# A graph attention block on one core: a step over eight elements instead of four, V through a second buffer, x in a ring of four

## The reference

```python
q, k, v = (heads(x @ W + b) for W, b in ((Wq, bq), (Wk, bk), (Wv, bv)))   # 6 heads of 64
scores = einsum('bhqd,bhkd->bhqk', q, k) / 8
probs = softmax(scores + where(adj, 0.0, -9e15)[:, None])
ctx = einsum('bhqk,bhkd->bhqd', probs, v)          # heads side by side again
x = x + ctx @ Wf + bf
out = (x - mean(x)) / sqrt(var(x) + 1e-5)          # over the 384 features
```

## Time and profile before

| | before |
|---|---|
| median of 3 runs | 1001.83 us (1001.54 to 1002.15) |
| profiled execution | 1002.12 us, span 1000.3 us |
| busy: PE / weight loads / DVE / ACT / POOL | 991.7 / 900.2 / 706.7 / 589.5 / 633.1 us |
| matmuls | 7690 |
| granted TensorE clock, mean | 0.999 |
| DMA | 178.08 MB, 178 GB/s, queue of SP busy 64.8% of 16 engines' span |

### The profile page before, as it was taken

How to read it: one execution, slowest core, us unless ns; L and a number is a source line. 1 busy time by engine, 2 the same in 40 slices (tenths; PEclk the granted TensorE clock), 3 DMA queues, 4 the chain that set the end, 5 groups by cost and what they waited for, 6 DMA issues and landing times.

```text
span 1000.3 us, 27877 instructions
## 1 busy us (share of the span) xinstructions
PE 991.7 (99%) x7690; PEld 900.2 (90%) x7690; DVE 706.7 (71%) x2760; ACT 589.5 (59%) x2130; POOL 633.1 (63%) x653
## 2 busy tenths in 40 slices
PE   9999999999999999999999999999999999999997
PEld 8788999889999889998899988999988999889997
DVE  5676766867668667677676686766777766867667
ACT  4766545675446665466654566554666545675556
POOL 2446657567566576575675765766656657567566
PEclk9999999999999999999999999999999999999999
DMA  8776676666776666766667666667666676665543
GB/s 186 175 196 167 172 210 189 178 163 171 199 193 186 168 170 175 218 172 182 161 176 204 188 178 169 173 183 207 181 173 168 171 215 181 176 171 160 160 151 104
DMA packets 344780, 178.08 MB, mean 178 GB/s; under 512 B 228784, under 2 KB 328752, under 8 KB 344752
## 3 DMA queue, kind: packets, MB, share of 16 engines
q1 hardware_dynamic: 343264, 176.77, 64.8%
q10 hardware_dynamic: 1488, 0.98, 0.3%
HBM read 103.35 MB, written 74.32 MB: 178 GB/s over the span
## 4 chain that ended last, share of the span: by engine, by line
PE 97%; ACT 1%; DVE 0%; DMA 0%; issue 0%; POOL 0%; SPq 0%; POOLq 0%; DVEq 0%
PE work_ps L427 16%; PE work_ps L429 15%; PE work_ps L428 15%; PE scores_ps L446 9%; PE scores_ps L466 9%; PE scores_ps L427 7%; PE scores_ps L429 7%; PE scores_ps L428 7%; PE work_ps L508 6%; PE scores_ps L508 6%; ACT probs L866 1%; DMA x_in<-in_x 0%; ACT qT L894 0%; PE scores_ps L545 0%; PE scores_ps L556 0%
## 5 line engine op out<-in xcount | busy, mean ns | idle before, releaser
L866 ACT ACTIVATE probs<-probs,neg_max 128x128 f32<-128x128 f32 x768 | 297.5, 392 | 87.9 <-DVE neg_max L676 87.9
L1038 POOL TENSOR_TENSOR probs<-probs,inv_sum 128x768 f32<-128x768 f32 x128 | 188.3, 1471 | 152.0 <-DVE inv_sum L699 152.0
L676 DVE CUSTOM_DVE_ANT_0 probs<-scores_ps,mask_bias 128x128 f32<-128x128 f32 x768 | 167.3, 286 | 127.9 <-PE scores_ps L446 127.2
L875 ACT COPY v_sb<-work_ps 128x384 f32<-128x384 f32 x128 | 61.3, 479 | 263.4 <-PE work_ps L429 263.4
L1033 POOL TENSOR_SCALAR y_sb<-y_sb,mean_var,rstd 128x384 f32<-128x384 f32 x120 | 198.4, 1653 | 21.5 <-POOL rstd L1023 21.5
L1023 POOL TENSOR_TENSOR rstd<-var_eps,minus_half 128x1 f32<-128x1 f32 x128 | 86.5, 676 | 168.5 <-DVE var_eps L720 168.5
L866 ACT ACTIVATION_READ_ACCUMULATOR probs<-probs,neg_max 128x1 f32 x768 | 146.9, 191 | 0.0
L1017 POOL TENSOR_TENSOR x_bias<-x_in,bias_row 128x384 f32<-128x384 f32 x128 | 128.9, 1008 | 7.7 <-DVE bias_row L829 7.7
L427 PE MATMUL scores_ps<-wf_hi,cT_hi 128*128 128x384 f32 x384 | 129.3, 337 | 0.0
L429 PE MATMUL scores_ps<-wf_hi,cT_lo 128*128 128x384 f32 x384 | 129.2, 336 | 0.0
L428 PE MATMUL scores_ps<-wf_lo,cT_hi 128*128 128x384 f32 x384 | 129.1, 336 | 0.0
(11 more groups left out here) (94 smaller groups left out, 2068.1 us busy)
## 6 DMA issues: line engine op xcount, KB each, us to landing
p_out<-p_turned SPq DMA_DIRECT2D x125, 384.0 KB, 2.8
pT<-p_out SPq DMA_DIRECT2D x500, 96.0 KB, 2.8
x_in<-in_x SPq DMA_DIRECT2D x128, 192.0 KB, 2.9
x_blocks<-in_x SPq DMA_DIRECT2D x372, 64.0 KB, 2.3
out<-y_sb SPq DMA_DIRECT2D x120, 192.0 KB, 2.1
adj_u<-in_adj SPq DMA_DIRECT2D x32, 64.0 KB, 2.1
out<-xT SPq DMA_DIRECT2D x4, 192.0 KB, 2.7
out<-qT SPq DMA_DIRECT2D x4, 192.0 KB, 1.9
```

Of the source, the lines that this page charges most:

```text
L676: last = nc.vector.tensor_tensor_reduce(out=probs[:, e, h, :], in0=scores_ps[:, score_cols(e, h)], in1=mask_bias[:, e, :], scale=-SCALE, s ...
L866: last = nc.scalar.activation(probs[:, e, h, :], probs[:, e, h, :], ACT.Exp, bias=neg_max[:, e, h:h + 1], scale=-1.0, accum_out=row_sum[:, ...
L1038: nc.gpsimd.tensor_tensor(probs[:, e, :, :], probs[:, e, :, :], inv_sum[:, e, :].unsqueeze(2).broadcast_to([P, HEADS, SEQ]), ALU.mult).the ...
```

## The change

A step now works on a set of eight elements (16 sets, one per turn of the loop). On PE it goes: scores of elements 0 to 3, two halved q/k products, scores of 4 to 7, two more halved products (four of twelve in all), the contexts of all eight, eight whole q/k products, then output products and V in fours. A context bank now holds one head pair of four elements instead of all heads of one, so `round_ctx` and `split_ctx` handle 128x512 tiles, three for four elements. x is transposed, rounded and split two elements at a time, the sums of elements 0 to 3 are inverted by one instruction. V is copied out of PSUM into `v_next` and moved to `v_sb` by four DMA transfers a step (`move_v`). `x_in` has four slots instead of eight, and POOL adds the bias in place; `x_blocks` has one slot instead of two. `y_sb` keeps four slots. In the last set nothing is transposed by PE, and its order on all engines is new. The pieces of the diff below are, in this order: buffers and banks, SP's new transfer, what the first scores of a set wait for on PE, PE's step, DVE's sum with x, POOL's step (its start and its end), and DVE's order in the last set.

```diff
-        x_in = sb("x_in", [P, RING, HID])
-        x_bias = sb("x_bias", [P, RING, HID])
-        x_blocks = sb("x_blocks", [P, TURN, KC, GROUP * BLOCKS, BLK])
+        x_in = sb("x_in", [P, GROUP, HID])
+        x_blocks = sb("x_blocks", [P, KC, GROUP * BLOCKS, BLK])
+        v_next = sb("v_next", [P, SET, HID])
+        v_sb = sb("v_sb", [P, SET, HID])
...
+OUT_BANKS = (2, 5, 6, 1, 7, 0, 3, 4)
+SCORE_PAIRS = (((0, 3), (1, 4), (2, 5)), ((1, 4), (2, 5), (6, 7)))
...
+            def move_v(s, q):
+                part = slice(2 * q, 2 * q + 2)
+                if q == 0:
+                    past(sp, v_copied, s * SET + SET - 1)
+                    past(sp, ctx_done, s * 2 * KC - 1)
+                sp.dma_start(v_sb[:, part, :], v_next[:, part, :]).then_inc(v_moved, DMA)
...
+                    elif pair == 0:
+                        past(pe, y_added, n - SET - 2)
+                    elif pair == 1:
+                        past(pe, y_added, n - SET - 1)
+                        past(pe, v_copied, n + 4)
...
+            def step(s):
+                if halved(s + 1):
+                    scores(s, 0)
+                    for j in (0, 1):
+                        qk_halves(s + 1, j)
+                scores(s, 1)
+                if halved(s + 1):
+                    for j in (2, 3):
+                        qk_halves(s + 1, j)
+                    for half in range(2):
+                        ctx_group(s - 1, half)
+                for j in range(HALVED if halved(s + 1) else 0, 2 * NJ):
+                    qk_product(s + 1, j)
+                for half in range(1 if is_step(s, LAST - 1) else 2):
+                    if not is_step(s, 0):
+                        for e in range(half * GROUP, (half + 1) * GROUP):
+                            out_product(s - 1, e)
+                    for e in range(half * GROUP, (half + 1) * GROUP):
+                        v_product(s + 1, e)
...
+            def add_residual(s, e):
+                n = s * SET + e
+                past(dve, out_done, n)
+                past(dve, x_biased, n)
+                if not is_late(n):
+                    past(dve, y_stored[e % GROUP], 2 * s + e // GROUP - 1, per=DMA)
...
+                    for e in range(GROUP):
+                        add_bias(s - 1, e)
+                    for e in range(SET):
+                        make_mask_bias(s + 1, e)
...
+                for e in (0, 1):
+                    normalise_y(s - 1, e)
+                for e in (4, 5):
+                    add_bias(s - 1, e)
+                normalise_y(s - 1, 2)
+                for e in (6, 7):
+                    add_bias(s - 1, e)
+                for e in range(3, GROUP if is_step(s, LAST - 1) else SET):
+                    normalise_y(s - 1, e)
...
+                turn_blocks(s, 6)
+                find_stats(s - 1, 1)
+                for m in range(KC):
+                    split_ctx(s - 1, 1, m)
```

More of the change, by code:

```diff
@@ L73, in past, with run_steps, is_step @@
     eng.wait_ge(sem, value)
[L76 to L85, removed]
+def run_steps(eng, step):
+    for s in range(FIRST_LOOPED):
+        step(s)
+    with eng.Fori(FIRST_LOOPED, END_LOOPED) as i:
+        step(i)
+    for s in range(END_LOOPED, LAST):
+        step(s)
+def is_step(s, n):
+    return isinstance(s, int) and s == n
 def attention_block(nc, x, adj, wq, bq, wk, bk, wv, bv, wf, bf, out):
@@ L199, in chunks, with split_ctx_at, tokens @@
+        def split_ctx_at(s, half):
+            if half and isinstance(s, int) and s >= LAST - 1:
+                at = s - LAST + 1
+                return xT_hi[:, at, :, :], xT_lo[:, at, :, :]
+            return cT_hi[:, :, :], cT_lo[:, :, :]
+        def tokens(e, count=1):
+            return slice(e % GROUP * SEQ, (e % GROUP + count) * SEQ)
         def chunks(ap):
@@ L444, in scores @@
+            def scores(s, half):
+                pe.wait_ge(qk_copied, copies(s, (half + 1) * NJ - 1))
+                if halved(s) and half == 0:
+                    pe.wait_ge(qk_summed, sums(s, HALVED - 1))
+                for e in range(half * GROUP, (half + 1) * GROUP):
                     for h in range(HEADS):
+                        t = e % GROUP * MATS + h // 2
+                        if t % 4 == 0 and h % 2 == 0:
+                            wait_for_score_pair(s, half, t // 4)
@@ L495, in qk_halves, with ctx_matmuls @@
-            def qk_halves(i, c, j):
-                mat, m = QK_JOBS[j]
-                n, cols = first_of(i, c), slice(m * P, (m + 1) * P)
+            def ctx_matmuls(s, e, m):
+                v = v_next if is_step(s, LAST) else v_sb
+                dst = ctx_bank(e // GROUP, m)
+                for half in range(2):
+                    h = 2 * m + half
+                    last = nc.tensor.matmul(dst[half * HEAD:(half + 1) * HEAD, tokens(e)],
+                                            v[:, e, h * HEAD:(h + 1) * HEAD], pT[:, e, :, h, :],
+                                            start=True, stop=True)
+                return last
@@ new lines, in copy_v, with copy_qk @@
+                nc.scalar.copy(v_next[:, e, :], v_bank(s, e)[:, 0:HID]).then_inc(v_copied, 1)
+            def copy_qk(s, j):
+                dst, col = job(j)
+                past(act, qk_done, s * 2 * NJ + j)
+                past(act, scores_done, (s - 1) * SET + j // NJ * GROUP + GROUP - 1)
+                if halved(s) and j < HALVED:
+                    nc.scalar.activation(dst, bank(HALF_PAIRS[j][0]), ACT.Identity, bias=col, scale=1.0
+                                         ).then_inc(half_copied, 1)
+                else:
+                    nc.scalar.activation(dst, qk_bank(s, j), ACT.Identity, bias=col, scale=1.0
+                                         ).then_inc(qk_copied, 1)
@@ L1084, in _ @@
+                for e in range(SET):
+                    add_bias(s, e)
+                for e in range(SET):
+                    normalise_y(s, e)
             beginning()
```

1273 lines of the change are left out of this document (741 added, 532 removed).

## The result

The changed kernel takes 1119.46 us (median of 4 runs, 1113.25 to 1121.32) against 1001.82 us: 1.116 times the time of before, 95% interval 1.112 to 1.121. The forecast had the direction and not the size: 1026 us, at most 1047. The profiled execution took 1113.25 us with a span of 1111.3.

A forecast was written before the change was run, and what follows sets the result against it. PE's own instructions were taken as the bound. Span 1000.3 - 4.2 - 2.2 - 1.5 + 5.1 - 0.8 = 996.7, plus 1.82 minus 0.29 gives 998.2; adding 13 x 2.1 gives 1025.5, said as 1026 us, range 1004 to 1047.

The forecast's parts named there:

- PE's own step, 61.06: PE, steady step of eight elements: fewer changes of matmul kind save 0.3 us, 61.36 to 61.06 us.
- The place and mechanism of the wait: PE, second third of the next scores: waits for element 7's sum, held by y of element 3's store; 0.5 to 3.7 us.
- So PE stands 2.1 us late.: PE at the scores: bank 4 free at 64.0, PE there at 61.95; 13 times, 27.3 us.
- the chain in front of it: From first scores through probabilities, SP's queue, x, biases and y's store to element 7's sum: 64.0 us.
- the bounds: Range of the 2.1 us wait: low 0.5, high 5 with all slow terms at once, 3.7 taken.
- 998.2: Whole kernel's time in us without the wait at the scores.
- The four V moves add no wait of their own ... but 1.8 us of the 25.3.: SP's queue: three V moves at 0.6 us take 1.8 of its 25.3 us; contexts want them a step later.
- The rival of transfers in each other's way: DMA: V moves' traffic and queued x loads make landings 3.75 us everywhere, 4 to 6 us a step; 1050 to 1076; 9%.
- A lower clock: PE: a lower granted clock after the new pauses, listed as a sign of being wrong, no size given.
- The ending, 5.1: Last set: output product of element 4 loses 4.1 us to a late context split, last splits about 1.0; bounds 0 and 6.
- The start, -1.5: First groups: half elements exponentiated between copies, so PE's 1.3 us stall goes; -1.5 us with the slower restart.
- Neither closes a longer circle.: POOL reaches next step's tile 0 at 13.7 us, wanted at 16; SP at 14.1, wanted at 19.

The follow-up runs named there:

- y of 2 and 3 first: Changed kernel with POOL normalising y of elements 2 and 3 ahead of the four biases of elements 4 to 7; 1071.3 us.
- V stays: Changed kernel with V moved to its second buffer for the first set only, later contexts computed from a wrong V (timing alone); 1041.3 us.
- the third kernel: Changed kernel with y, x, sums and splits reordered, V moved from ACT's queue behind all exponentials, x split before the inversion, nothing left out of the computation; 1011.7 us.
- third, V stays: The third kernel with V moved for the first set only, later contexts computed from a wrong V (timing alone); 1004.9 us.
- small moves: Changed kernel with V moves of 12 KB instead of 393 from the second set on, same queue places and waits (timing alone); 1074.2 us.

## Where the forecast was right, and where it failed

- **PE's own step, 61.06.** Right: 61.1. The saving over the 61.36 of before is there and small, as said.
- **The place and mechanism of the wait.** Right for the second third of the scores, to the releaser, the number of steps and the part of the chain behind x; even its size there, 1.8 us a step, is near the 2.1. Not forecast was the wait for the sum of element 6 at the first scores, 2.5 us a step: only the last link was compared with PE's arrival, and the 1.4 us in hand at the link before were not looked at. y of 2 and 3 first, the cheapest cure, gave back 48 us.
- **"So PE stands 2.1 us late."** The step that failed. The waits at the scores are 4.3 us (55.8 / 13), and a step loses 7.6. The mis-sized term is the chain in front of it, 69.0 instead of 64.0. In the chain above, 1.75 and 0.9 us come from V moves and a tile store that lands late, 1.05 from DVE and POOL side by side, 1.7 for the most part from the clock. In the bounds I had varied single landings, not what runs beside what. Their upper sum was wrong besides: 0.45 + 0.85 + 0.8 + 1.5 on top of 2.1 is 5.7, not 5. Even that, 998.2 + 13 x 5.7 = 1072, is below what came, as the clock is in none of the terms.
- **"The four V moves add no wait of their own ... but 1.8 us of the 25.3."** They add no wait of their own, but 1.8 failed: they lengthen the chain by 4.0 us, and with what follows from that the places cost 33 us and the bytes another 45. The rival of transfers in each other's way (1050 to 1076, 9%) was closer to the truth than the forecast, and 1119 is beyond it too; its sign was read off a median landing that V moves were not yet in.
- **A lower clock** stood in the list of what would show me wrong, without a price. It should have been a term. It cost 24 us through the chain, and it goes with PE's busy time being 33 us longer. One pause of the forecast size alone might have been free of it: in *V stays*, with one pause of 0.8 to 2.0 us a step, the clock stayed at 2.4 GHz.
- **The ending, 5.1.** Its wait is there (4.3 us for the split of set 14's second half), and so is one that I had not seen, 5.4 us at the last set's V product of element 4, held by the sum of element 6 of set 13. **The start, -1.5:** 0.41 is left of the 1.3 us, but V's product waits 2.1 for a copy, so nothing is won.
- **"Neither closes a longer circle."** Right for POOL and SP: in the changed kernel each waits at the next set's tile 0 for the engine before it (POOL 1.86 us for DVE's inversion).

The shares (24, 33, 45, 48, 57 us) sum to more than 118, because they are cures of one loop: whichever shortens it first takes the clock's part with it.

What stays open: the last 10 us (7 to 13) by which the third kernel is slower than the one before, though its step is 0.2 us shorter. 7 of them go with V's moves: three of its steps take 62.4 to 62.8 us instead of 61.0, with 3.6 us of PE's waits for DVE's masks. The other 3, and the 3.4 that thirteen steps of 61.1 save, are lost in the start and the ending, where PE still waits 3.3 us for the last tiles; an ending of its own was not tried. Even with V's move for nothing, then, the order over eight elements is not faster.

## What to carry to other kernels

When a wait is the difference of two long sums, price the sums' neighbours before the wait: what runs beside each operation now that did not before, and which landings something waits for. Compare every wait on the way with its deadline, not the last alone. Pauses of PE in a steady loop are to be entered with the time at 1.2 GHz that can follow. Here two of 1.9 and 2.2 us with sixteen scores between them were followed by 1.2 GHz, one of about 2.6 in most steps, one of up to 2.0 in *V stays* was not. Each us of wait that an order took away at the scores gave about 2 us (48 for 21.7, 57 for 26.9, 45 for 21.0). And an order that makes a ring of slots shorter should hand the slot back first: put the instruction that frees it ahead of those that wait for DMA.

## What the runs showed that I had not expected

- The granted clock fell to 1.2 GHz within the sixteen scores between two pauses and stayed there for 3.4 us of full work behind the second; filling 3.2 us of the pauses with idle transposes kept it at 2.4, and so did having one pause of up to 2.0 us instead of two.
- A split of 128x768 with two SBUF inputs that began during POOL's scaling took 2.23 us, one that began first 0.94; POOL's two tiles beside them took 2.10 and 2.18 instead of 1.47.
- A transfer of 393 KB issued from ACT's queue in every step landed in 4.4 to 5.3 us, the same from SP's in 3.2. It is not the queue by itself: in *third, V stays*, where ACT issues four of them in the first set alone, they landed in 2.8.
- Waits of 90 us in total (ACT for V) were worth nothing, and a wait with 1.1 us in the trace of before (DVE for the store of a tile) grew to 113.7 us (74.3 with small moves).
